# Expert stage of a gated attention and mixture-of-experts block: the second layer one step later, the gated product in a ring of four

## The reference, cut to what matters

```python
x = x + tanh(g_xattn[0]) * xattn(layernorm(x), ctx, ctx, Wq, Wk, Wv, Wp, bp)   # 16 heads, rotary on k and v
x = x + tanh(g_ffn[0]) * ffn(layernorm(x), gate, w0, w1, wo)

def ffn(x, gate, w0, w1, wo):                      # x: (128, 64, 128), 8192 tokens
    logits = einsum('ble,en->bln', x, gate)        # 8 experts
    top_w, top_i = top_k(logits, 2)
    weights = scatter(softmax(top_w), top_i)
    mult = silu(einsum('ble,neh->blnh', x, w0)) * einsum('ble,neh->blnh', x, w1)   # hidden 256
    return einsum('blne,bln->ble', einsum('blnh,nhe->blne', mult, wo), weights)
```

## Time and profile before

| | before |
|---|---|
| median of the timed runs | 548.91 us (548.64 to 549.88, three runs) |
| profiled execution, span from first to last instruction | 665.6 us |
| busy in the span: TensorE, its weight loads | 561.5, 468.0 us |
| busy: VectorE, ScalarE, GpSimd | 393.9, 431.8, 384.0 us |
| mean granted TensorE clock in the profiled execution | 0.971 |
| instructions | 21070 |

### The profile page before, as it was taken

How to read it: one execution, slowest core, us unless ns; L and a number is a source line. 1 busy time by engine, 2 the same in 40 slices (tenths; PEclk the granted TensorE clock), 3 DMA queues, 4 the chain that set the end, 5 groups by cost and what they waited for, 6 DMA issues and landing times.

```text
span 665.6 us, 21070 instructions
## 1 busy us (share of the span) xinstructions
PE 561.5 (84%) x6123; PEld 468.0 (70%) x6124; DVE 393.9 (59%) x1418; ACT 431.8 (65%) x1090; POOL 384.0 (58%) x524
## 2 busy tenths in 40 slices
PE   8998898998989899899898779787778978888960
PEld 6886676776767677677776668676677868877860
DVE  6797787777778677677778643372133323223663
ACT  4897787887787788788777735344244546556540
POOL 3347756576575666657566466575545555545651
PEclk9999999999999999999999899897899999999995
DMA  3801111111111111111112112233222222225996
GB/s 91 240 20 57 42 42 52 36 55 40 48 44 36 56 40 48 48 33 58 41 55 63 33 50 73 64 98 101 85 64 80 77 74 76 76 68 174 270 272 206
DMA packets 64242, 52.98 MB, mean 80 GB/s; under 512 B 8607, under 2 KB 60064, under 8 KB 64176
## 3 DMA queue, kind: packets, MB, share of 16 engines
q1 hardware_dynamic: 46560, 30.79, 16.5%
q0 software_dynamic: 8448, 16.93, 7.7%
q10 hardware_dynamic: 9168, 4.46, 2.3%
HBM read 29.44 MB, written 23.22 MB: 79 GB/s over the span
## 4 chain that ended last, share of the span: by engine, by line
PE 51%; another core or an unknown queue 15%; issue 10%; ACT 8%; DVE 6%; ACTq 3%; DMA 2%; DVEq 2%; POOL 1%; SPq 1%; POOLq 0%
PE psK L583 10%; PE psH L603 8%; PE psH L483 5%; PE psH L489 4%; PE psG L498 4%; PE psH L498 3%; PE psK L471 3%; ACT wcur L757 3%; PE psO L619 2%; ACTq L319 2%; ACT ys L771 2%; PE psK L619 2%; ACT hs L764 2%; PE psO L518 2%
## 5 line engine op out<-in xcount | busy, mean ns | idle before, releaser
L1251 POOL DMA_INDIRECT results<-ys,zin x136 | 136.1, 1001 | 106.5 <-ACT ys L771 68.3
L603 PE MATMUL psH<-zT,wcur 128*128 128x128 f32 (+1 forms) x760 | 139.1, 333 | 20.1 <-ACT wcur L757 15.2
L1178 POOL DMA_INDIRECT lists<-zp,dest x128 | 129.6, 1012 | 34.8 <-issue 31.1
L603 PEld LDWEIGHTS psH<-zT,wcur 128*128 128x128 f32 x760 | 112.8, 195 | 34.4 <-ACT wcur L757 20.1
L1083 DVE TENSOR_TENSOR hm<-psH,hs 128x512 f32<-128x512 f32 x68 | 47.0, 692 | 121.0 <-remote 45.7
L977 DVE TENSOR_REDUCE mx<-psH 128x8 fp32r<-128x512 f32 x128 | 82.5, 686 | 43.4 <-PE psH L483 23.6
L696 ACT ACTIVATE ex<-psH,rs 128x512 f32<-128x512 f32 x128 | 86.8, 688 | 23.9 <-PE psH L489 16.3
L583 PEld LDWEIGHTS psK<-v,pT 128*64 128x64 f32 x2048 | 69.6, 137 | 37.1 <-issue 36.3
L583 PE MATMUL psK<-v,pT 128*64 128x64 f32 x2048 | 81.1, 226 | 9.0 <-issue 8.6
L757 ACT COPY wcur<-w 128x512 f32 x95 | 56.1, 619 | 15.2 <-issue 14.2
L747 ACT COPY v<-kvr 64x64 f32<-64x64 f32 x256 | 63.7, 249 | 2.2
(11 more groups left out here) (176 smaller groups left out, 1140.5 us busy)
## 6 DMA issues: line engine op xcount, KB each, us to landing
yy<-results SPq DMA_DIRECT2D x16, 512.0 KB
zin<-lists SPq DMA_DIRECT2D x41, 130.0 KB
out_dram<-x ACTq DMA_DIRECT2D x16, 256.0 KB
xring<-in_x_dram SPq DMA_DIRECT2D x31, 128.0 KB
cring<-in_ctx_dram SPq DMA_DIRECT2D x31, 128.0 KB
zin<-lists SPq DMA_DIRECT2D x54, 65.0 KB
results<-ys,zin POOLq DMA_INDIRECT x136
w<-in_L_ffn_w_kernel_dram SPq DMA_DIRECT2D x2, 1024.0 KB, 7.1
```

What stands on the lines that cost most here:

```text
L603: last = pe.matmul(bank[t.buf(2)][:, k * ET + c.start:k * ET + c.stop], wcur[:, t.buf(2), h, a, k * P:(k + 1) * P], zT[:, t.buf(2), c], st ...
L1178: nc.gpsimd.indirect_dma_start(lists, bass.IndirectOffsetOnAxis(ap=dest[:, t.buf(4), j:j + 1], axis=0), zp[:, t.buf(4), j, :], None).then_ ...
L1251: nc.gpsimd.indirect_dma_start(results, bass.IndirectOffsetOnAxis(ap=zin[:, t.buf(8), h, D:D + 1].bitcast(U32), axis=0), ys[:, t.buf(8), h ...
```

## The change

In the step order, a tile's second layer on TensorE and the copies of its result on ScalarE are moved from step t to step t+1: `second_layer` and `outputs` now work on tile s-1. The pipeline therefore has one more step behind the last tile (`behind=2`), and all that was placed in a given step next to a certain second layer is moved by one step: the last routing tile's products on TensorE, the second table and the combines on VectorE. hm lives longer and gets a ring of four buffers in place of two; VectorE's wait before it writes hm goes back four tiles. At the start of the stage the calls for tile 0's second layer and copies are dropped, and the order of a few routing operations on VectorE is another. SyncE's and GpSimd's instruction lists are the same as before.

```diff
-EXPERTS = Pipeline(NET, behind=1, ahead=2, unroll=8, steady=18, turns=2)
+EXPERTS = Pipeline(NET, behind=2, ahead=2, unroll=8, steady=18, turns=2)
-COMBINE_AT = NET + 1 - CHUNKS_EARLY
+COMBINE_AT = NET + 2 - CHUNKS_EARLY
...
-        hm = sb("hm", [P, 2, 2, ET])
+        hm = sb("hm", [P, 4, 2, ET])
...
                 def second_layer(s):
-                    if t := EXPERTS.at(s, 0):
+                    if t := EXPERTS.at(s, -1):
                         e = [expert(pe, t, h) for h in range(2)] if late(t) else [expert(pe, t)] * 2
                         wait_for(pe, h_done, t)
                         wait_for(pe, y_sb, t, back=2)
...
-                                last = pe.matmul(psY[t.buf(2)][:, h * D:(h + 1) * D], hm[:, t.buf(2), k, h * P:(h + 1) * P],
+                                last = pe.matmul(psY[t.buf(2)][:, h * D:(h + 1) * D], hm[:, t.buf(4), k, h * P:(h + 1) * P],
...
-                pe.wait_ge(on_done, NT)
-                second_layer((None, 0))
-                for n in (x1_done, oT_sb):
+                for n in (on_done, x1_done, oT_sb):
                     pe.wait_ge(n, NT)
                 EXPERTS.run(pe, experts_step, since=1)
...
                 def outputs(s):
-                    if t := EXPERTS.at(s, 0):
+                    if t := EXPERTS.at(s, -1):
                         wait_for(act, y_ps, t)
                         wait_slot(act, y_out, t, 32, back=8)
...
-                outputs((None, 0))
...
-                        wait_for(dve, y_ps, t, back=2)
-                        nc.vector.tensor_tensor(hm[:, t.buf(2), :, :].rearrange("p k t -> p (k t)"), psB[t.buf(2)][:, :], hs[:, t.buf(2), :],
+                        wait_for(dve, y_ps, t, back=4)
+                        nc.vector.tensor_tensor(hm[:, t.buf(4), :, :].rearrange("p k t -> p (k t)"), psB[t.buf(2)][:, :], hs[:, t.buf(2), :],
...
-                        second_table(s[1] - 7)
+                        second_table(s[1] - 8)
...
                 experts_step((None, 2))
+                experts_step((None, 3))
+                means(Tile(8, None, NT - 1))
                 rows(Tile(8, None, NT - 1), psO)
-                experts_step((None, 3))
+                experts_step((None, 4))
                 hits(Tile(8, None, NT - 1))
                 row_weights(Tile(8, None, NT - 1))
                 destinations(Tile(8, None, NT - 1))
-                means(Tile(8, None, NT - 1))
-                EXPERTS.run(dve, experts_step, since=4)
+                EXPERTS.run(dve, experts_step, since=5)
```

More of the change, by code:

```diff
@@ L612, in second_layer @@
                         wait_for(pe, y_sb, t, back=2)
-                        if static(s, 3):
+                        if static(s, 4):
                             pe.wait_ge(place_done, NT)
-                        if static(s, 7):
+                        if static(s, 8):
                             pe.wait_ge(late_table, 1)
@@ L628, in experts_step @@
                     second_layer(s)
-                    if static(s, 2):
+                    if static(s, 3):
                         pe.wait_ge(y_sb, 2)
                         places(Tile(8, None, NT - 1), psO)
-                    if static(s, 6):
+                    if static(s, 7):
                         pe.wait_ge(y_sb, 6)
```

## The result

The changed kernel takes 554.11 us (median of 11 runs, 552.98 to 557.55); the kernel before, in the same runs, 549.38 us (548.64 to 552.86). The ratio is 1.0082, 95% interval 1.0064 to 1.0099: slower by 4.5 us (3.5 to 5.4). The forecast was +2.0 us. The direction was right, and the forecast size was less than half of what was measured.

What follows compares the result with a forecast made beforehand. Timed runs were taken to be paced by TensorE's own work; -0.5 (hm wait) + 0 (beginning) + 1.6 (end) + 0.9 (loads) = +2.0 us, from 548.9 to 550.9 us, with an 8-in-10 range of 545.2 to 554.3 us.

Steps and rivals of the forecast that it cites:

- What bounds the kernel: Both stages: timed runs are paced by TensorE's own work, 4.81 us attention and 2.84 us expert steps.
- The hm wait: Before L619, expert stage: removing waits for hm gains between 0 and 5.5 us, taken as -0.5 us.
- The beginning: First expert tiles: 0.98 us of waits removed, 0.9 us of work left over; taken as 0, bounds -0.5 and +0.9.
- The steady state: Middle of the expert stage: copies keep their relation to TensorE, other engines see the same step length; 0 us.
- The end: After the last L603: GpSimd's queue holds three tiles' scatters instead of two; +1.6 us, bounds 0 and +1.8.
- credit of 0.9 us: End of stage: the scatter row starts 0.9 us earlier, with one second layer less ahead of the last L603.
- The loads of zin: Last 16 tiles: SyncE's loads go out a step later and fall short; +0.9 us, bounds 0 and +3.7.
- Stalls real: Rival: TensorE's signals also come late in timed runs, so removed hm waits win; 544.8 us, 20%.
- Hidden anyway: Rival: DMA traffic, not GpSimd's issue, bounds the last results, so the end stays; within 1 us of 548.9, 17%.
- Loads too late: Rival: zin's longer round trip stalls TensorE at the stage's end and between 400 and 500 us; 553.4 to 554.2 us, 16%.
- the forecast's own range: Whole kernel: the main forecast of 550.9 us, between 549.3 and 552.8 us, given 47%.

Runs made afterwards that it cites:

- ring_only: The kernel before with only hm's ring of four and VectorE's wait four tiles back, second layer and copies unmoved: ratio 1.0009, +0.5 us.
- before_scatters_late: The kernel before with only GpSimd's scatters one step later, waiting for the next tile's results' copy: ratio 1.0076, +4.2 us on before.
- delayed_from_36: The changed kernel, but second layers and results' copies stand as before until step 35 and one step later from step 36: ratio 1.0069, +3.8 us on before.
- after_spare_slots: The changed kernel with eight more zin slots, so loads of tiles 60 to 67 wait for no scatter or copy: ratio 1.0078, +4.3 us on before.
- catching up at step 60: The changed kernel doing two tiles' second layers and copies in step 60, then keeping the old order for them: ratio 1.0058, +3.2 us on before.
- undoing both from step 40 on: The changed kernel doing two tiles' second layers and copies in step 40, then the old order, with before's combines: ratio 1.0032, +1.8 us on before.

## Why the prediction came out as it did

**What bounds the kernel: right.** The profile's excess was kept out of the sum because a timed run had no room for it. The second profile has steps of mostly 4.81 us in the attention (4.88 in the mean) and of 2.84 to 2.90 us in the undisturbed part of the expert stage, close to those taken from the earlier trace rows. The share of weight loads, which the Trainium skill (Perfetto Trace Analysis, Identifying the Most-Contended Engine) prefers to the busy share of matmuls, is 83% there (453.0 of 546.9 us). In the expert stage it agrees that TensorE is full (49.6 of 50.0 us from 440 to 490 us); in the attention it is 84% (167.2 of 200 us from 100 to 300 us), although matmuls fill 199.2 us of the same stretch. The distance of an instruction from one tile to the next was the better measure.

**The hm wait, -0.5: worth nothing.** One wait of 0.65 us existed. It was replaced by a wait of 1.09 us of the instruction that came into its place. The rows at the first second layer, before and after:

```profile
330.14 1.15 PE L619 MATMUL psK<-wo,hm 128*128 x8 [0.65 <-DVE hm L1083]
331.13 0.38 PE L592 MATMUL psG<-ident,zin 128*128 128x128 f32 x2
331.35 1.89 PE L603 MATMUL psH<-zT,wcur 128*128 128x256 f32 x8
```

```profile
330.15 0.41 PE L592 MATMUL psG<-ident,zin 128*128 128x128 f32 x2 [1.09 <-issue]
330.40 1.94 PE L603 MATMUL psH<-zT,wcur 128*128 128x256 f32 x8
```

**The beginning, 0: a lead that did not last.** TensorE resumes at 330.15 instead of 330.14 us. As its stream was 0.43 us ahead, it resumes 0.44 us later by its own clock. The row names no releaser; that it is x1_done, as predicted, fits x being written until 329.83 us, and is not shown. L603 is 0.95 us earlier, of which 0.52 us belong to the change. Counted from tile 0 the changed kernel is 0.65 us ahead at tile 8 and 0.20 us behind at tile 29. In between, from tile 9 to 25, where GpSimd works off its list scatters, TensorE waits for zin in both kernels (2.4 us in four waits, before 2.1 in two). This part can take up a lead or a delay: ring_only comes to it 1.4 us late and leaves it 0.07 us ahead of before (before_scatters_late comes as late and keeps 1.1 us). A layer left out behind it, in step 36 of delayed_from_36, stays a lead of 0.7 us. That waits for loads took the lead in the changed kernel is the likely reading of this and was not tested alone.

**The steady state, 0: right.** From tile 29 to tile 62 the distance between the two kernels does not change by more than 0.01 us. The rival's "clearly slower between 400 and 500 us" has no row for it.

**The end, +1.6: too small, measured +2.7 in the profile.** The mechanism was as described: three tiles of scatters in one row instead of two, +2.56 us. What failed is the credit of 0.9 us "because one second layer less stands ahead of the last L603". Counted from L592 of the last tile, the row starts at the same distance, 8.42 and 8.43 us, and what the left-out layer had gained ahead of that was gone at tile 29. The prediction's own beginning, in which L592 and L603 keep nearly their times, had no such lead to give either.

**The loads of zin, +0.9: too small, between 1.3 and 2.9 us in the profile.** The late stretch is +2.9 us (+1.6 against ring_only, whose profile had 1.3 of it); 1.3 us is one named wait for a load, at tile 64, and after_spare_slots, whose loads wait for no slot, has +0.5. The working gave a shortage of 0.65 to 3.7 us, and I took the end near the 2.0 us landing of the earlier trace rows, a row of the program's first loads. The loads concerned land in full DMA queues. In the changed kernel, 440 to 490 us first, then 497 to 520 us:

```profile
DMA to landing us min/median/max: 1.8/1.9/2.7
...
DMA to landing us min/median/max: 2.5/3.3/4.3
```

The Trainium skill (DMA: Bandwidth & Descriptors, Latency and other measured facts) puts HBM access at 0.2 us on average and 2 us at high load, and calls it the main part of a transfer's fixed cost. The rows above go the same way (the median grows by 1.4 us under load); that HBM access is the cause no run here shows.

Also the wait was put down to the copies and the scatters alike; the runs point to the scatters (shifting SyncE's wait for the copies back gains nothing, delaying the scatters alone costs 4.2 us). SyncE issues the loads of tile 64 (the first line of each pair) 2.84 us later, about one step, though TensorE was still 0.23 us ahead at tile 62. Before, then after:

```profile
504.24 0.86 SPq L388 DMA_DIRECT2D zin<-lists  x2
505.16 0.44 SPq L395 DMA_DIRECT2D yy<-results  x1
```

```profile
507.08 0.86 SPq L388 DMA_DIRECT2D zin<-lists  x2
508.00 0.47 SPq L395 DMA_DIRECT2D yy<-results  x1
```

Put together, the profiles have +0.2 us from tile 0 to 59, where the forecast's -0.5 and its credit of -0.9 made -1.4; +2.9 in the late stretch, where it had +0.9; and +2.7 at the end, where its row of scatters had +2.6. Less the 0.4 us that the stream was ahead at tile 0, this is the +5.4 of the spans. It describes one execution of each kernel, and was put together afterwards.

**The rivals.** Stalls real: refuted by the second profile. Hidden anyway: refuted, the end moved with GpSimd's queue. Loads too late: of the three it came nearest. Its price, 1.6 us at the end and one step or up to 3.7 us of loads, gave 553.4 to 554.2 us, and 554.11 were measured; nothing of it showed between 400 and 500 us, and in the profile less than half of the late stretch is a named wait for a load. It had been given 16%. The wide range held the time because it had been drawn for the rivals too; the forecast's own range, with its 47%, did not.

**What stays open.** In the profiles the late stretch and the end look like two terms that add. In the timed runs catching up at step 60, which undoes the end, gives back 1.3 us (4.5 to 3.2), and undoing the late loads alone 0.2 us (4.5 to 4.3), while undoing both from step 40 on gives back 2.7. Each of these differences is uncertain by about 1.4 us. after_spare_slots shows one reason why they need not add: what TensorE wins, GpSimd's row takes. How much of the 4.5 us is each one's alone was not settled, nor what the rest of the late stretch is made of where no load is named. None of the kernels beat the one before.

## What to carry to other kernels

When work is moved by one step, follow every consumer's queue to the end of the stage: here TensorE had nothing to gain (steps without a gap) and the last engine in line, GpSimd, with 2.6 us of scatters for each tile, had one tile more to work off when its supply ended. Keep one clock for all terms, such as one engine's instruction per tile, and measure each term from it. A lead counts only if it reaches the end: here 0.65 us were ahead at tile 8 and gone at tile 29, past a part of the stage where loads made TensorE wait, while a lead won behind that part stayed. And take the latency of a transfer from rows under the same load: 1.9 us in the quiet part was 3.3 us where the queues were full.

## What the runs showed of the hardware

A profiled execution can be 21% longer than the timed ones of the same program (665.6 us against 548.9), with the busy times of VectorE and ScalarE within 4 us of the second profile's and a chain full of an "unknown queue"; profiled again, the kernel spans 546.9 us. The sign was that the span did not fit the timed runs.

GpSimd's issue of an indirect scatter takes 0.98 us nearly always, but 1.33 us (before_scatters_late) and 1.49 us (after_spare_slots) for single ones at the end of the stage. There the DMA engines are busy for 0.89 of the time instead of 0.35, as the last but one figure of these lines of before_scatters_late says (after the length of the stretch, the engines' busy times and the granted clock); that the one comes from the other is not shown:

```profile
440.00:490.00 50.00, 50.00 (x428) 49.38 (x428) 17.58 (x35) 37.68 (x85) 33.95 (x35) 1.00 0.35 96
490.00:530.00 40.00, 36.85 (x316) 35.38 (x316) 24.19 (x43) 26.61 (x61) 24.06 (x25) 1.00 0.89 263
```
